# Constant bf16 products on TensorE behind the scores of the first five slots of each dense attention

## The reference, cut to what matters

```
scores = q @ k.T / sqrt(8)            # causal mask in mqa only
probs  = softmax(scores)
y      = probs @ v                    # then an output projection and a residual
```

## Time and profile before

| | us |
|---|---|
| median of three runs | 4435.36 |
| lowest, highest | 4432.89, 4436.02 |
| the profiled execution's own time | 4448.09 |
| its span, first to last instruction | 4446.4 |
| TensorE busy | 4257.4 (96%) |
| VectorE busy | 3200.7 (72%) |
| ScalarE busy | 2674.1 (60%) |
| GpSimd busy | 2128.0 (48%) |
| mean granted clock of TensorE | 0.968 of full |

### The profile page before, as it was taken

The page is one execution under the profiler, slowest core; times in us unless marked ns, Lnnn a source line. Parts: engine busy times, 40 slices in busy tenths (PEclk is TensorE's granted clock), DMA queues, the critical chain, the costliest instruction groups (busy, mean ns, idle before and its releaser), DMA issues.

```text
span 4446.4 us, 148531 instructions
## 1 busy us (share of the span) xinstructions
PE 4257.4 (96%) x66660; PEld 2391.6 (54%) x66660; DVE 3200.7 (72%) x4171; ACT 2674.1 (60%) x3161; POOL 2128.0 (48%) x1151
## 2 busy tenths in 40 slices
PE   8998999869999999999999997899999999999998
PEld 4543433334555555555555553555555565555555
DVE  3565666466787787777777766777787787777874
ACT  1452355324676676676776761576776776776774
POOL 0110000014666666666666650666666665666663
PEclk8899899979999999999999998999999999999999
DMA  2000000001112111111111111111111112121111
GB/s 85 1 2 1 1 1 1 1 0 41 33 33 56 32 33 55 33 54 34 32 55 34 29 33 51 29 29 34 54 33 36 52 33 55 33 58 30 33 33 29
DMA packets 78741, 144.96 MB, mean 33 GB/s; under 512 B 18656, under 2 KB 25120, under 8 KB 76576
## 3 DMA queue, kind: packets, MB, share of 16 engines
q1 hardware_dynamic: 78112, 135.45, 11.8%
HBM read 39.97 MB, written 1.05 MB: 9 GB/s over the span
## 4 chain that ended last, share of the span: by engine, by line
PE 82%; POOL 7%; DVE 6%; ACT 2%; issue 2%; DMA 0%; SPq 0%; POOLq 0%; DVEq 0%; ACTq 0%
PE psum L1329 13%; PE psum L1381 7%; PE psum L1354 7%; PE psum L1342 6%; PE psum L1298 5%; PE psum L1400 5%; PE psum L687 5%; PE psum L1312 4%; PE psum L1430 3%; POOL arena L1776 3%; PE psum L1446 3%; PE psum L1440 3%; PE psum L1395 3%; PE psum L719 3%; PE psum L741 3%; POOL arena L1782 2%
## 5 line engine op out<-in xcount | busy, mean ns | idle before, releaser
L1776 POOL TENSOR_TENSOR arena<-arena 128x1024 f32<-128x1024 f32 x384 | 722.2, 1902 | 875.4 <-ACT arena L1524 875.4
L1770 POOL TENSOR_TENSOR arena<-arena 128x1024 f32<-128x1024 f32 x384 | 907.5, 2363 | 234.9 <-DVE arena L1645 234.9
L1641 DVE TENSOR_TENSOR arena<-psum,arena 128x1024 f32<-128x1024 f32 x384 | 467.6, 1218 | 599.6 <-ACT arena L1517 599.4
L1517 ACT ACTIVATE arena<-psum 128x1024 f32<-128x1024 f32 x384 | 392.0, 1021 | 266.1 <-PE psum L1329 266.1
L1381 PEld LDWEIGHTS psum<-arena 64*64 64x64 f32 x24576 | 397.0, 135 | 214.0 <-issue 213.9
L1530 ACT ACTIVATE arena<-psum 128x1024 f32<-128x1024 f32 x384 | 390.5, 1017 | 199.1 <-PE psum L1342 199.1
L1645 DVE TENSOR_TENSOR arena<-psum,arena 128x1024 f32<-128x1024 f32 x384 | 466.2, 1214 | 0.0
L1652 DVE TENSOR_REDUCE h_pair<-arena 128x16 f32<-128x1024 f32 x384 | 464.1, 1209 | 0.0
L1381 PE MATMUL psum<-arena 64*64 64x32 f32 x24576 | 439.6, 221 | 7.2 <-DVE arena L1619 5.2
L1342 PE MATMUL psum<-w_ident,arena 128*128 128x128 f32 x3072 | 415.5, 278 | 17.7 <-POOL arena L1776 10.1
L1342 PEld LDWEIGHTS psum<-w_ident,arena 128*128 128x128 f32 x3072 | 337.9, 141 | 151.4 <-POOL arena L1776 84.7
(11 more groups left out here) (268 smaller groups left out, 7043.7 us busy)
## 6 DMA issues: line engine op xcount, KB each, us to landing
arena<-arena SPq DMA_DIRECT2D x672, 128.0 KB, 2.4
deep_wqkv<-in_deep_wqkv SPq DMA_DIRECT2D x6, 1536.0 KB, 7.1
arena<-in_deep_wqkv SPq DMA_DIRECT2D x6, 1536.0 KB, 7.2
arena<-arena SPq DMA_DIRECT2D x96, 64.0 KB, 2.0
deep_wo<-in_deep_wo SPq DMA_DIRECT2D x6, 512.0 KB, 7.5
arena<-in_deep_wo SPq DMA_DIRECT2D x6, 512.0 KB, 7.4
deep_w<-in_deep_w SPq DMA_DIRECT2D x6, 341.0 KB, 7.6
arena<-in_deep_w SPq DMA_DIRECT2D x6, 341.0 KB, 7.6
```

What stands on the lines that cost most here:

```text
L1641: nc.vector.tensor_tensor(turned[:, hs, :].rearrange("p h (a e) -> p h a e", a=2), swapped, sin, ALU.mult).then_inc(de.deep_rope_parts, 1)
L1770: nc.gpsimd.tensor_tensor(roped[a % 2][:, hs, :], roped[a % 2][:, hs, :], turned[:, hs, :], ALU.add).then_inc(de.deep_summed, 1)
L1776: nc.gpsimd.tensor_tensor(roped[a % 2][:, hs, :], roped[a % 2][:, hs, :], over(h_inv[a % 2][:, hs], [P, LHEADS, LD]), ALU.mult).then_inc(d ...
```

## The change

In each half of slots 0 to 4, after the scores (and after the turn of the maxima in slot 4), TensorE makes two of the constant products into bank 7. That is 4 products a slot, 20 for each dense attention, 40 in all.

```diff
@@ -762,6 +762,8 @@ def dense_attend_pe
                         dense_mix_pe(pe, causal, i - mix_lag(causal), half, N)
                     if half == 0 and turn_of(i) is not None:
                         dense_max_pe(pe, i, N)
+                    if i < LAG:
+                        busy_pe(2, bank(7))
```

## The result

The changed kernel takes 4459.73 us, the kernel before 4436.15 us (medians of 12 runs each). The ratio is 1.0049, 95% interval 1.0032 to 1.0065: 0.49% slower, some 22 us, where 2.7 us faster had been forecast. The time lies outside the range that was given (4421 to 4443 us). It is nearest the second rival: 19.4 us over the kernel before, 4454.8 us.

What follows compares the result with a forecast made beforehand. The prediction took TensorE as the bound, so added work could help only through the clock. mqa -12.2 and rope +9.5 summed to -2.7 us, taking the median 4435.36 to 4432.7 us, range 4421 to 4443.

Steps and rivals of the forecast that it cites:

- the second rival: Products don't hold the clock in mqa and run at half speed: mqa +9.9, with rope +19.4 us, 4454.8 us; chance 0.08.
- Why the clock would hold in `mqa`: mqa enters at clock 1.00; products put one or two full-array matmuls into every microsecond where it fell, so it holds.
- mqa in all -12.2: Sum over mqa's first twelve slots, +0.5 - 5.4 - 7.3 = -12.2 us, between -6.4 and -15.1.
- mqa, to the turn: mqa's slots 0 to 3 and the turn, all at full clock: 10.2 instead of 9.72 us, +0.5; ends -1.2 and +3.5.
- mqa, the next four slots: mqa from the first turn to the turn four slots on: 10.4 instead of 15.76 us at full clock, -5.4.
- The four after: mqa's four slots after its second turn: 13.19 instead of 20.45 us at full clock, -7.3.
- rope, to the turn: rope from first score to turn, products at half clock: 23.9 instead of 14.32 us, +9.6 if the clock stays low.
- now a slot is 2.92 us: rope's slot before the change, read as 11.39 us of 28 scores' instructions spread over slots 1 to 4.
- rope, after the turn: Behind rope's turn: clock rises some 2 us after it, -1.4, last four products +1.3: -0.1, or +3.5 if later.
- The first rival: Clock rises early in rope's slots, then about 2.75 us a slot: rope +0.3, net -11.9, 4423.5 us; chance 0.16.
- The prediction's worry: The profiled execution lies 12.7 us above the median; if part is longer half clock in mqa, the gain there is smaller.

## Why the prediction was wrong

The step that failed is "Why the clock would hold in `mqa`". It rested on the clock's coming in at 1.00 "after 10.24 us with hardly a pause", and on the products being dense from the first score on. The row ahead of the score was read too coarsely. The timeline of the changed kernel shows what stands at its end: eight instructions of 32 columns and a pause, and only then scores of 128 columns and the first products.

```profile
118.69 0.97 PE L619 MATMUL psum<-arena 64*128 64x32 f32 x8
120.09 0.61 PE L687 MATMUL psum<-arena 32*128 32x128 f32 x4 [0.43 <-DVE arena L874]
120.64 0.61 PE L155 MATMUL psum<-maskb,identb 128*128 128x512 bf16 x2
121.17 0.49 PE L687 MATMUL psum<-arena 32*128 32x128 f32 x4
121.59 0.60 PE L155 MATMUL psum<-maskb,identb 128*128 128x512 bf16 x2
```

At 122.14 us the clock was gone, though four products had run at full clock by then. With four more ahead of the score it held in three executions of three; how they did it is the open point named above. The term "mqa in all -12.2" measured +10.1. With the products ahead it was -10.7 (the first score itself then starts about 0.5 us later), so its sizes were about right and its condition, a clock that holds, was not met.

- mqa, to the turn: +0.5 forecast, +8.2 measured. At full clock, with the products ahead, +1.5: 11.2 us against my 10.2, inside its ends of 8.5 and 13.2.
- mqa, the next four slots: 10.4 us forecast, 17.7 measured, and 10.8 where the clock held. The four after: 13.19 forecast, 20.42 measured, and 13.2 where it held.
- rope, to the turn: +9.6 forecast, +11.6 measured. The mechanism was right, the size short: a pair takes 2.01 us, not 1.9, and two products 0.96, not 0.86. I had left out about 0.1 us at each change between 32-row and 128-row matmuls. VectorE's wait of 3.4 us a slot is near the 3 that had been forecast. A reading was wrong beside it: "now a slot is 2.92 us" is VectorE's pace; the 28 instructions that it names are those of 3.5 slots, so 3.2 us each.
- rope, after the turn: -0.1 forecast, +0.8 measured; the clock came back 4.1 us after the turn's start (576.3 against 572.16), where I had taken 2.
- The first rival (clock rises early in rope) did not come; the clock stayed at 0.50 for all of slots 0 to 3 in each of the four profiled kernels with two 128- or 64-row products a pair that entered slot 0 at 0.50. That it would stay low was right, against the plain reading of the rule in the Trainium skill (TensorE: Matmul & The Clock Gate, "What's actually happening"): TensorE was busy for 25.91 of 25.91 us, at 0.50. The rival's 2.75 us a slot at full clock was too small as well: with the clock at 1.00 throughout, a slot took 3.2 us.
- The second rival is what happened. Its figures were 17.9 us to the turn (measured 17.9), 1.7 for the last four products (2.0) and 9.5 in rope (12.4): 19.4 against 22.5. Its chance of 0.08 was too low. What had been known for certain was that the clock fell there in the one execution shown, and between that case and mine lay 22 us in mqa alone, eight times the gain forecast.

The prediction's worry that the profiled 4448 us might overstate mqa's loss stays open: the kernel before has times from 4427 to 4458 us with a gap between 4435 and 4445 in one group of 35 runs, and which stretch makes the difference was not found. The end of `mqa`, at half clock in some profiled executions and not in others, is a candidate with about 9 us.

## What to carry to other kernels

In this kernel, products that were to keep the clock up had to stand ahead of the first score as well as behind it; without those ahead, the others ran at half speed and cost twice. Give such products a shape with which they lie beside the work around them, and look in the timeline whether they do: two 32-row products a pair made this kernel faster where two 128-row ones made it slower, and 64-row ones did not overlap. And price the case in which the clock is not held before counting on the one in which it is.

## What the runs showed of the hardware that was not expected

- A 64-row product and 32-row matmuls on the other 64 rows did not overlap (2.01 us for the pair and 0.96 for the two products, as with 128 rows), while 32-row products on rows 96 to 127 did. Only this pairing of sizes and types was tried, and the scores behind the 64-row products use the same rows as these.
- TensorE was busy in every microsecond and stayed at 1.2 GHz for 33.6 us in mqa of the kernel before, where the scores and keys use 32 rows of the array and the mixes 32 columns, and for 25.91 us in rope of the changed one. In mqa the 32-row products brought the clock back 24.5 us earlier; the 64-row ones, without those ahead, did not (50.0 us after the first score, against 43.3 before the change). So in this kernel the busy share of the profile does not tell where the clock goes.
- Two products between pairs of 32-row scores took 0.96 us from start to start at half clock, where two in a row of their own take 2 x 0.43, and 0.53 us at full clock, against 2 x 0.216. An estimate from these: some 0.1 us for the change between the two shapes, at either clock.
